# Square and cube on VectorE ahead of th_lo in an RK4 scan with an overlapped FFN

## The reference, cut to what matters

```
dq = q - q**3/3 - p + drive + tanh(q) @ coupling.T + bias
dp = 0.08 * (q + 0.7 - 0.8*p)
# four evaluations (k1..k4), q_next = clip(q + DT/6*(k1+2k2+2k3+k4)), p likewise; q_next is the output of the step
probs = softmax(x @ W_router.T); top 2 -> combine
shared = (silu(x@Ws_gate) * (x@Ws_up)) @ Ws_down * sigmoid(x @ W_sgate.T)
sparse = sum over experts of combine[e] * ((silu(x@We_gate[e]) * (x@We_up[e])) @ We_down[e])
out = x0 + shared + sparse
```

## Time and profile before

| what | value |
|---|---|
| time, median of 3 runs (lowest, highest) | 680.31 (679.57, 681.56) |
| the profiled execution: its own time, its span | 681.01, 679.2 |
| busy: PE, PEld, DVE, ACT, POOL | 637.4 (94%), 603.2 (89%), 617.7 (91%), 402.2 (59%), 181.7 (27%) |
| instructions | 33795 |
| mean granted TensorE clock | 0.995 |
| first and last q of the scan (L760), count | 10.7 to 651.1, 512 |
| what L895 on POOL waited for most | DVE's force, 287.5 in 217 times |

### The profile page before, as it was taken

One profiled execution on the slowest core, in us unless ns is written; L12 is line 12 of the kernel. 1 busy time (PEld: TensorE's weight loads), 2 busy tenths in 40 slices (PEclk: granted clock), 3 DMA queues, 4 the chain that ended last, 5 costly groups with the idle time before them and its releaser, 6 DMA issues.

```text
span 679.2 us, 33795 instructions
## 1 busy us (share of the span) xinstructions
PE 637.4 (94%) x12779; PEld 603.2 (89%) x12779; DVE 617.7 (91%) x4190; ACT 402.2 (59%) x2244; POOL 181.7 (27%) x404
## 2 busy tenths in 40 slices
PE   3657999999999999999999999999999999999998
PEld 2446899999999999999999999999999999999997
DVE  6798999999999999999999999999999999998961
ACT  2766565656566565656656565656656565664653
POOL 0001023232322323232232323222232322323243
PEclk9999899999999999999999999999999999998999
DMA  8700000000000000000000000000000000000000
GB/s 301 255 1 2 3 3 3 11 4 11 3 12 3 3 12 3 12 2 12 4 2 11 3 11 3 12 4 2 12 3 12 3 11 4 2 12 3 11 3 17
DMA packets 8627, 13.65 MB, mean 20 GB/s; under 512 B 1520, under 2 KB 7984, under 8 KB 8208
## 3 DMA queue, kind: packets, MB, share of 16 engines
q1 hardware_dynamic: 8464, 11.50, 5.0%
HBM read 9.40 MB, written 2.10 MB: 17 GB/s over the span
## 4 chain that ended last, share of the span: by engine, by line
DVE 67%; PE 19%; issue 7%; ACT 3%; DMA 2%; SPq 0%; POOL 0%; DVEq 0%; POOLq 0%
DVE th_lo L735 10%; DVE hidden L816 9%; DVE force L753 8%; DVE p_sum L707 7%; DVE cubic L738 7%; PE up_ps L563 6%; PE down_ps L578 5%; DVE q L760 5%; DVE y L707 5%; DVE q_raw L760 3%; DVE rest L707 3%; PE coup_ps L511 3%; PE coup_ps L505 2%; DMA wf<-in_w_up 2%; DVE w L695 2%
## 5 line engine op out<-in xcount | busy, mean ns | idle before, releaser
L563 PE MATMUL up_ps<-q_hi,w 128*128 128x128 f16 x2176 | 239.0, 221 | 0.2 <-POOL q_lo L863 0.2
L895 POOL TENSOR_TENSOR hidden<-hidden,comb_s 128x128 f32<-128x128 f32 x272 | 123.3, 456 | 328.8 <-DVE force L753 287.5
L389 ACT ACTIVATE th_hi<-q 128x32 f16<-128x32 f32 x384 | 88.0, 229 | 197.3 <-DVE q L760 195.2
L563 PE MATMUL up_ps<-q_lo,w 128*128 128x128 f16 x1088 | 202.1, 221 | 0.0
L505 PE MATMUL coup_ps<-th_hi,c 128*128 128x16 f16 x4096 | 181.9, 171 | 2.7 <-ACT th_hi L389 2.7
L578 PE MATMUL down_ps<-hidden,wd 128*128 128x128 f32 x1088 | 180.3, 289 | 0.0
L563 PEld LDWEIGHTS up_ps<-q_hi,w 128*128 128x128 f16 x2176 | 177.7, 98 | 0.4 <-POOL q_lo L863 0.4
L505 PEld LDWEIGHTS coup_ps<-th_hi,c 128*128 128x128 f16 x4096 | 139.7, 97 | 8.7 <-ACT th_hi L389 3.5
L578 PEld LDWEIGHTS down_ps<-hidden,wd 128*128 128x128 f32 x1088 | 142.0, 191 | 0.0
L511 PE MATMUL coup_ps<-th_lo,c 128*128 128x16 f16 x2048 | 131.1, 172 | 9.5 <-DVE th_lo L735 6.5
L494 PE MATMUL coup_ps<-xb,ident_u 128*128 128x32 bf16 x512 | 93.4, 182 | 21.2 <-DVE q L760 14.6
(11 more groups left out here) (93 smaller groups left out, 1079.5 us busy)
## 6 DMA issues: line engine op xcount, KB each, us to landing
wf<-in_w_up SPq DMA_DIRECT2D x1, 4224.0 KB, 13.9
wd<-in_w_down SPq DMA_DIRECT2D x1, 2048.0 KB, 22.8
out<-out_s SPq DMA_DIRECT2D x16, 128.0 KB, 2.2
xs<-in_x SPq DMA_DIRECT2D x1, 1920.0 KB, 19.4
sel<-in_spread SPq DMA_DIRECT2D x1, 408.0 KB, 18.9
cf<-in_coupling SPq DMA_DIRECT2D x1, 256.0 KB, 2.6
xs<-in_x SPq DMA_DIRECT2D x1, 128.0 KB, 2.5
ident<-in_identity SPq DMA_DIRECT2D x1, 64.0 KB, 2.5
```

The source lines that it names most:

```text
L563: last = nc.tensor.matmul(up_ps[(f * TILES + j) % UPS][:, h * TOK:(h + 1) * TOK], w16[:, part, k, h, j * P:(j + 1) * P], q[:, k, :], start ...
L895: nc.gpsimd.tensor_tensor(hidden[:, j, :], hidden[:, j, :], comb_s[:, j, :], ALU.mult).then_inc(weighed, 1)
```

## The change

In stages with k = 1, 2, 3, ACT no longer computes the square. DVE computes `square` = (c/3) q q into SBUF and then `cubic`, both ahead of th_lo, and the helper sum (y3, rest3, rest4) moves in front of the wait for q, that is, directly behind the previous stage's q. `prepare` and `slot`, with all FFN work of DVE, move behind force, between force and the next q. Stages with k = 0 keep their order, with ACT's square. Besides: the padding is at most 6 matmuls; eight extra matmuls run in each stage of the second half of block 0; the abs-sum and what follows from it (`HI_AT`, `LO_AT`) start one stage later, with two of the w_lo steps now in stages 23 and 24 of block 1; the bias and the splits for block 1 move one and two stages later; and split_x uses scalar_tensor_tensor with a factor of 1.0 where it used tensor_tensor.

```diff
-SQUARE = [math.sqrt(c / 3.0) for c in C]
+SQUARE = math.sqrt(C[0] / 3.0)
+THIRD = [c / 3.0 for c in C]
-WARM = [max(0, 11 - units(st)) for st in range(STAGES)]
+WARM = [min(6, max(0, 11 - units(st))) for st in range(STAGES)]
 W_PARTS = 8
-SUM_AT = 6
+SUM_AT = 7
-         + [STAGES + s for s in (0, 1, 2, 3, 4, 6, 7, 9, 10, 16, 17)])
+         + [STAGES + s for s in (0, 1, 2, 3, 4, 6, 7, 9, 10, 16, 17, 23, 24)])
-X_FIRST = [14, 15]
+X_FIRST = [15, 16]
-SPLIT_NEXT = [15, 16, 17, 18]
+SPLIT_NEXT = [17, 18, 19, 20]
...
                     if t:
 
                         act.wait_ge(q_clipped, t)
-                    q = q0_of(st // 4)
-                else:
-                    q = q[:]
-                nc.scalar.activation(square, q, ACT.Square, scale=SQUARE[st % 4]).then_inc(squared, 1)
+                    nc.scalar.activation(square_first, q0_of(st // 4), ACT.Square, scale=SQUARE).then_inc(squared, 1)
 
             def ffn(f, st):
                 if st == 0:
...
                         pe.wait_ge(in_const, 4 * 16)
                     for f, at in ffn_stages(b, st)[::-1]:
                         ffn(f, at)
+                    if b == 0 and st >= STAGES // 2:
+
+                        for _ in range(8):
+                            nc.tensor.matmul(up_ps[0][:, 0:P], c16[:, 0, 0, 0:P], c16[:, 0, 0, 0:P], start=True,
+                                             stop=True)
 
             blocks(one_block)
             for f, at in tail_stages():
...
                 steps = slice(first, first + HALF)
                 if part % 2 == 0:
                     dve.wait_ge(x_biased, KC * (b + 1))
-                    op = nc.vector.tensor_tensor(flat(x_rest, steps), flat(xb, steps), upper(xb, steps), ALU.subtract)
+                    op = nc.vector.scalar_tensor_tensor(flat(x_rest, steps), flat(xb, steps), 1.0,
+                                                        upper(xb, steps), ALU.mult, ALU.subtract)
                 else:
                     dve.wait_ge(x_split, 4 * b + part)
-                    op = nc.vector.tensor_tensor(flat(x_low, steps), flat(x_rest, steps), upper(x_rest, steps),
-                                                 ALU.subtract)
+                    op = nc.vector.scalar_tensor_tensor(flat(x_low, steps), flat(x_rest, steps), 1.0,
+                                                        upper(x_rest, steps), ALU.mult, ALU.subtract)
                 op.then_inc(x_split, 1)
 
             split_x(0, 0)
...
                     if i == 1 and b:
                         dve.wait_ge(q_split, (KC + 1) * b)
                     nc.vector.tensor_scalar(q, q_raw[:], CLAMP, -CLAMP, ALU.min, ALU.max).then_inc(q_clipped, 1)
-                prepare(n)
-                slot()
+                if k == 0:
+                    prepare(n)
+                    slot()
+                elif k == 1:
+                    add(y3[:], p_now[:], P_IN_Y3, q0_of(i))
+                elif k == 2:
+                    add(rest3[:], q_in[1][:], R3_Q2, y3[:])
+                else:
+
+                    dve.wait_ge(y4_ready, t + 1)
+                    add(rest4[:], q_in[2][:], R4_Q3 / R4_Q1, y42[:])
                 if k:
                     dve.wait_ge(q_ready, n)
-                if k == 1:
-                    add(y3[:], p_now[:], P_IN_Y3, q0_of(i))
+                    nc.vector.scalar_tensor_tensor(square[:], q, THIRD[k], q, ALU.mult, ALU.mult).then_inc(squared, 1)
                     add_to_p()
-                elif k == 2:
-                    add_to_p()
-                    add(rest3[:], q_in[1][:], R3_Q2, y3[:])
-                elif k == 3:
-                    add_to_p()
-                    add(rest4[:], q_in[2][:], R4_Q3 / R4_Q1, y42[:])
-
+
+                    dve.wait_ge(squared, n + 1)
+                    nc.vector.scalar_tensor_tensor(cubic[:], square[:], LINEAR[k], q, ALU.subtract, ALU.mult
+                                                   ).then_inc(cubed, 1)
                 mid()
 
                 dve.wait_ge(tanh_ready, n + 1)
                 nc.vector.tensor_tensor(th_lo[:], th, th_hi[:], ALU.subtract).then_inc(lo_ready, 1)
-
-                dve.wait_ge(squared, n + 1)
-                nc.vector.scalar_tensor_tensor(cubic[:], square, LINEAR[k], q, ALU.subtract, ALU.mult
-                                               ).then_inc(cubed, 1)
                 if k == 0:
+
+                    dve.wait_ge(squared, n + 1)
+                    nc.vector.scalar_tensor_tensor(cubic[:], square_first, LINEAR[k], q, ALU.subtract, ALU.mult
+                                                   ).then_inc(cubed, 1)
                     add(p_sum[:], p_now[:], P_NEXT, q)
-                elif k == 1:
-                    add(y4[:], p_now[:], P_IN_Y4, q0_of(i))
-                elif k == 2:
-                    add(y42[:], q_in[1][:], R4_Q2 / R4_Q1, y4[:])
-                else:
-
-                    dve.wait_ge(p_summed, t * 3 + 3)
-                    nc.vector.tensor_scalar(p_now[:], p_sum[:], P_HIGH, P_LOW, ALU.min, ALU.max)
 
                 dve.wait_ge(cubed, n + 1)
                 rest, factor = ((p_now, -Q_NEXT[0]), (v1, R2_Q1), (rest3, 1.0), (rest4, R4_Q1))[k]
                 nc.vector.scalar_tensor_tensor(force[:], rest[:], factor, cubic[:], ALU.mult, ALU.subtract
                                                ).then_inc(summands, 1)
-                late()
                 if k == 0:
                     add(v1[:], p_now[:], P_IN_V1, q)
+                elif k == 1:
+                    add(y4[:], p_now[:], P_IN_Y4, q0_of(i))
+                elif k == 2:
+                    add(y42[:], q_in[1][:], R4_Q2 / R4_Q1, y4[:]).then_inc(y4_ready, 1)
+                else:
+
+                    dve.wait_ge(p_summed, t * 3 + 3)
+                    nc.vector.tensor_scalar(p_now[:], p_sum[:], P_HIGH, P_LOW, ALU.min, ALU.max)
+                if k:
+                    prepare(n)
+                    slot()
+                late()
 
                 dve.wait_ge(summands, 2 * (n + 1))
                 nc.vector.scalar_tensor_tensor(
```

More of the change, by code:

```diff
@@ L180, in program @@
         th_lo = sb("th_lo", [P, KC, B], F16)
+        square = sb("square", [P, KC, B])
         cubic = sb("cubic", [P, KC, B])
@@ L219, in program @@
         square_ps = pb("square_ps")
-        th, square = [ps[:, 0:CB].rearrange("p (m b) -> p m b", m=KC) for ps in (th_ps, square_ps)]
+        th, square_first = [ps[:, 0:CB].rearrange("p (m b) -> p m b", m=KC) for ps in (th_ps, square_ps)]
         comb_tp = route_ps[0:96, 64:128].bitcast(BF16)
@@ L250, in program @@
         p_summed = sem("p_summed")
+        y4_ready = sem("y4_ready")
         parted = sem("parted")
```

## The result

| | before | after |
|---|---|---|
| time, median of 4 runs each (lowest, highest) | 680.39 (679.57, 681.56) | 720.85 (719.32, 722.27) |
| the profiled execution: its own time, its span | 681.01, 679.2 | 719.32, 717.5 |
| first and last q | 10.7, 651.1 | 10.6, 689.3 |
| mean granted TensorE clock | 0.995 | 0.967 |

The changed kernel takes 1.060 times as long (95% interval 1.058 to 1.062), 40 us more. The forecast was 713.2 with a range of 698 to 728: side and mechanism are right, and the point is 7.6 low.

A forecast was written before the change was run, and what follows sets the result against it. DVE's order around th_lo was taken to set nearly every window's time. The profiled 681.0 us, +33.5 for blocks 2 to 15 (+2.39 each), -2.0 for the start and +0.7 for block 1 gave 713.2, range 698 to 728.

The forecast's parts named there:

- free window: Windows 5, 13 and 15, without GpSimd beside them: 1.18 us instead of 1.21, together -0.06 a block.
- 0.12 a stage: Block 0: without ACT's Square the abs-sums of six stages follow sooner, by 0.12 us each, -0.7 together.
- The hold: Behind q, GpSimd's multiplication holds rest to 0.36 us; twelve plain windows a block take 1.32 for 1.21, +1.32.
- A: Rival: GpSimd doesn't hold rest at 0.17, th_lo stays at 0.64; +0.03 us per block, total 680; chance 12%.
- D: Rival: rest behind q is held half as long, passing at 0.27 us; -24, total 689; chance 6%.
- B: Rival: rest is held for GpSimd's whole record; +36 us more, total 750; chance 3%.
- x_rest: Split step, now behind force with GpSimd done: 0.29 us; its scalar_tensor_tensor form costed at nothing, bounds 0 to +0.06.
- The waits: PE for hidden: windows 12, 14, 19, +0.16, +0.17, +0.29 us; routing result: window 7 +0.30, window 8 +0.10.
- The start: First blocks: later abs-sum -0.9 us, sooner abs-sums -0.7, later x_rest -0.6, w_lo +0.3; together -2, bounds 0 to -3.
- Block 1: No weighs until stage 16; held windows and late w_lo against smaller padding and possibly warmer PE: +0.7 us, bounds 0 to +1.5.
- rival C: PE clock falls oftener, as padding shrinks and windows lengthen: 14 falls at 1.0 us, +14, total 727; chance 14%.

The follow-up runs named there:

- experiment 9: Kernel before with only the edits of the first blocks (abs-sum, w_lo, bias and splits for block 1 later): 678.73 us, ratio 0.9965 to 0.9986.
- experiment 11: Kernel before with padding of at most six, the edits of the first blocks and the later blocks' splits moved away from GpSimd's multiplication: 670.74 us.
- experiment 1: Changed kernel with GpSimd's multiplication cut to 8 of 128 columns, the routing weight of the other 120 left out: 684.69 us, ratio 1.0049 to 1.0078.
- experiment 7: Changed kernel without the eight extra matmuls in each late stage of block 0: 721.07 us, ratio 1.0578 to 1.0615 to the kernel before.
- experiment 6: Changed kernel with padding back at up to eleven matmuls: 725.28 us, ratio 1.0649 to 1.0702 to the kernel before.
- experiment 8: Kernel before with padding capped at six matmuls: 676.16 us, ratio 0.9922 to 0.9962.
- experiment 3: Changed kernel with prepare and slot back in front in every stage, square and cubic left ahead of th_lo: 732.81 us, ratio 1.0748 to 1.0779.
- experiment 10: Kernel before with the splits of blocks 2 to 15 moved to stages that GpSimd's multiplication leaves alone: 676.91 us, ratio 0.9921 to 0.9950.
- experiment 4: Changed kernel with four PSUM banks for up products instead of three, the square of k = 0 stages going to SBUF: 716.73 us, ratio 1.0520 to 1.0550.

## Why the prediction was right, and where it was off

*The bound.* DVE's order between q and th_lo set the time, as the prediction read from the earlier trace rows. Taking ACT's square away gave next to nothing in blocks 2 to 15, where th_lo waits for th_ps and not for the square: 0.02 to 0.03 in each free window, which comes from cubic and force being done earlier. In block 0 the forecast had priced it at 0.12 a stage, and windows 10 to 12, with an abs-sum in each, take 1.31 where they take 1.42 or 1.43 in the kernels of experiments 9 and 11, which kept the square; these kept DVE's order too, so its share alone isn't shown.

*The hold.* The term that carried the forecast, +0.11 in each of twelve windows, measured +0.12: the window is 1.33, not 1.32. rest lasts 0.378 in the trace against 0.181 undisturbed, so it is released 0.197 later than it starts, at 0.168 + 0.197 = 0.365 behind q. GpSimd's record ends at 0.50: 0.135 before that, as the earlier trace rows gave (forecast: 0.36 and 0.13). Window 22 excludes the rivals: A, that it doesn't bite, wanted 1.19, D, half of it, 1.23, and B, the whole record, 1.46. Experiment 1 ties the hold to GpSimd's multiplication. The Trainium skill, SBUF — State Buffer, "Who interferes with whom", is borne out in that the two contend. That the first keeps the ports for its whole instruction, which the page says of this very case in its section "SBUF: two separate sides", is not borne out, if GpSimd's record is its instruction; but records of POOL are rough at their ends.

*x_rest* behind force, in its new form:

```profile
384.56 0.28 DVE L662 SCALAR_TENSOR_TENSOR x_rest<-xb 128x128 f32<-128x128 f32 x1
```

0.28, as costed at nothing against the earlier trace rows.

*The waits.* All were where they were named: hidden releasing PE in stages 11, 13 and 18, which_f in stage 7, prob in stage 8. Their sizes were off by little: 12, 14 and 19 measured 1.31, 1.35 and 1.54 (forecast 1.37, 1.37, 1.50), window 8 1.28 (1.31), window 1 1.37 (1.39). Together these are 0.08 under the forecast and the smaller groups 0.03 over it; with the plain windows' 0.14 the block is 0.09 over, 1.2 us in fourteen.

*The start.* -2.4 for -2.0, although the eight extra matmuls, which the forecast took for nothing, took 0.47 of the gain away (experiment 7). Block 1 measured +1.8 for +0.7: its windows 3 and 8 are 0.54 and 0.38 shorter, and its seven plain held windows from 21 on 0.12 longer each. But windows 12 and 19, behind up waits, are 0.38 and 0.41 longer, window 13 is 0.27 longer, and windows 17 and 23, where w_lo now stands between force and q (0.48, and 0.35 behind x_rest), are 0.21 and 0.26 longer. The forecast priced block 1 by its missing GpSimd work, did not add its up waits, and took w_lo behind force for too little.

*The clock.* This is the term that was off most. The sum took no fall of the granted clock, by the earlier trace rows, and gave rival C, fourteen falls at 1.0, 14%. It was neither: five blocks of fourteen, at 0.65 to 1.57 each, and the one fall of before. That is 3.8 of the 7.6 us missing, at about C's price and a third of its count. Of C's two reasons one is refuted: less padding is not it (experiments 6 and 8). Longer windows remain. Over blocks 2 to 15 PE is busy 558.3 of 587.6 us (95.0%) in the changed kernel and 541.5 of 549.0 (98.6%) in the kernel before. In one profiled execution each, the six kernels with the change's held windows (the changed one, experiments 3 to 7) show a fall in 5, 4, 3, 6, 7 and 4 of these 14 blocks; the other eight show 1 to 3, experiment 1 with 2 and experiment 10 with 3 among them. That is a correlation. No experiment changed the window length alone with all else equal, and the cause of single falls stays open. The Trainium skill, TensorE: Matmul & The Clock Gate, Part 1, has activity release the higher clock, and these counts agree in direction.

The whole gap: the sum was made for the profiled execution, which took 719.3, so it is 6.1 short there. Clock 3.8, windows 1.2, block 1 1.1, start -0.4 make 5.7, and 0.4 isn't assigned. The other 1.5 is the distance of that execution, the fastest of its four, to their median.

## What to carry to other kernels

Before an instruction with two SBUF inputs is moved on VectorE, look what GpSimd does at its new place, not how long it lasts in its old one: here the filler that read PSUM had been standing in exactly the time in which GpSimd holds up such an instruction, and it cost nothing there. Work moved behind the last instruction of the critical chain is not free if another engine waits for it; list its readers (a bank to be freed, an index result with two readers) and price each. A step added ahead of the last operand must be weighed against who is really late there: the engine relieved here, ACT, was idle 41% of the time.

## What the runs showed of the hardware that was not expected

- ACT's 128x32 square takes 0.21 to SBUF and 0.18 to PSUM, and the dependent window grows from 1.207 to 1.237 (experiment 4).
- A routing step of 128x8 (TENSOR_SCALAR with two per-partition operands) is held by GpSimd's multiplication like the larger ones: 0.36 in experiment 3 and in the kernel before, against 0.285 in the changed one.
- GpSimd's multiplication of 128x8 still lasts 0.20, against 0.46 for 128x128, and a rest that starts 0.12 into it isn't held (experiment 1).
- In blocks 2 to 15 of every trace the stretches at the lower clock come at the same place of the block: they begin in windows 1 to 3 and lengthen window 3, window 4 or both, with 6 or with 11 padding matmuls.
